# Local attention: the weighted product in front of masks and scores, masks as quarter products

## The reference

```python
q = l2norm(q) * qs;  k = l2norm(k) * ksc
q, k = rotary_xpos(q, k)
# windows of 64 queries; keys of the own window and of the one before
sim = einsum('bhwid,bhwjd->bhwij', bq, bk)
mask = (i < j) | (i > j + WINDOW) | (j == -1)
sim = where(mask, -finfo.max, sim)
attn = softmax(sim, axis=-1)
out = einsum('bhwij,bhwjd->bhwid', attn, bv)
x = x + out.reshape(b, n, INNER) @ wo
```

## Time and the profile before

| | before |
|---|---|
| median of three runs | 1756.01 us (1754.92 to 1756.5) |
| profiled execution, own time | 1755.7 us |
| its span, first to last instruction | 1753.9 us |
| mean granted TensorE clock | 0.991 |
| PE busy | 1674.9 us (95%) |
| PE weight loads (PEld) | 1154.1 us (66%) |
| DVE busy | 1446.5 us (82%) |
| ACT busy | 1299.2 us (74%) |
| POOL busy | 1039.0 us (59%) |
| DMA, mean | 54 GB/s |

### The profile page before, as it was taken

One profiled execution on the slowest core, in us unless ns is written; L12 is line 12 of the kernel. 1 busy time (PEld: TensorE's weight loads), 2 busy tenths in 40 slices (PEclk: granted clock), 3 DMA queues, 4 the chain that ended last, 5 costly groups with the idle time before them and its releaser, 6 DMA issues. The chain is left out here.

```text
span 1753.9 us, 54573 instructions
## 1 busy us (share of the span) xinstructions
PE 1674.9 (95%) x18245; PEld 1154.1 (66%) x18373; DVE 1446.5 (82%) x3283; ACT 1299.2 (74%) x3588; POOL 1039.0 (59%) x1015
## 2 busy tenths in 40 slices
PE   6999999979999999999989997999999999998997
PEld 4666666646777777777765664777777777775664
DVE  3777777769999999999967776899999999986996
ACT  5888888848998998989982224998998998985221
POOL 1333333337777777777763324777777777775664
PEclk9999999989999999999999999999999999999999
DMA  3211111111111111111113321111111111113443
GB/s 118 69 48 48 48 48 48 43 43 35 44 39 39 42 40 37 42 42 36 42 50 94 92 76 37 38 43 45 33 42 45 33 42 45 33 40 88 110 122 86
DMA packets 201095, 94.02 MB, mean 54 GB/s; under 512 B 82578, under 2 KB 192060, under 8 KB 201020
## 3 DMA queue, kind: packets, MB, share of 16 engines
q1 hardware_dynamic: 201020, 93.06, 20.1%
HBM read 51.00 MB, written 25.23 MB: 43 GB/s over the span
## 5 line engine op out<-in xcount | busy, mean ns | idle before, releaser
L846 ACT ACTIVATE pr<-banks,nb,rr 128x128 f32<-128x128 f32 x1024 | 456.3, 465 | 5.0 <-DVE nb L915 5.0
L747 POOL TENSOR_TENSOR rr<-ss,half_neg 128x16 f32<-128x16 f32 x128 | 374.4, 2925 | 19.0 <-POOL ss L744 17.0
L764 POOL TENSOR_TENSOR pr<-pr,rl 128x512 f32<-128x512 f32 x256 | 266.5, 1041 | 103.3 <-DVE rl L877 103.3
L885 DVE TENSOR_REDUCE ss<-sq 128x16 f32<-128x1024 f32 x128 | 156.1, 1219 | 75.4 <-ACT sq L795 61.3
L846 ACT ACTIVATION_READ_ACCUMULATOR pr<-banks,nb,rr 128x1 f32 x1024 | 216.5, 211 | 0.0
L1216 ACT ACTIVATE f_g<-banks,b_s 128x512 f32<-128x512 f32 (+1 forms) x96 | 65.9, 686 | 202.0 <-PE banks L1300 192.2
L893 DVE TENSOR_REDUCE mx<-banks 128x8 f32<-128x1024 f32 x128 | 156.0, 1219 | 9.0 <-PE banks L1022 8.3
L383 POOL TENSOR_SCALAR a_ve<-a_mv 128x2 f32<-128x2 f32 x96 | 21.4, 223 | 226.5 <-DVE a_mv L394 223.4
L755 POOL TENSOR_TENSOR krot<-ka,rr 128x512 f32<-128x512 f32 x128 | 134.4, 1050 | 22.3 <-POOL rr L747 11.7
L974 PE MATMUL banks<-ident,pr 128*128 128x128 f32 x1024 | 141.2, 281 | 5.9 <-POOL pr L764 5.9
L837 ACT COPY pT<-banks 128x512 f32<-128x512 f32 x128 | 75.1, 587 | 95.9 <-PE banks L974 95.9
(11 more groups left out here) (126 smaller groups left out, 4210.4 us busy)
## 6 DMA issues: line engine op xcount, KB each, us to landing
ve<-vt SPq DMA_DIRECT2D x128, 128.0 KB, 2.2
hs<-y_d SPq DMA_DIRECT2D x128, 64.0 KB, 2.0
yt<-y_d SPq DMA_DIRECT2D x64, 128.0 KB, 2.1
y_d<-yn SPq DMA_DIRECT2D x64, 128.0 KB, 2.0
f_h<-y_d SPq DMA_DIRECT2D x128, 64.0 KB, 2.0
f_y<-y_d SPq DMA_DIRECT2D x64, 128.0 KB, 2.2
xa<-in_L_attn_x SPq DMA_DIRECT2D x32, 128.0 KB, 2.2
xr<-in_L_attn_x SPq DMA_DIRECT2D x32, 128.0 KB, 2.3
```

Of the source, the lines that this page charges most:

```text
L747: nc.gpsimd.tensor_tensor(rr[:, r, :], ss[:, r, :], half_neg[:], ALU.pow).then_inc(T["rr"], 1)
L764: nc.gpsimd.tensor_tensor(pr[:, e], pr[:, e], rl[:, e].unsqueeze(2).broadcast_to([P, UH, P]), ALU.mult).then_inc(T[("ne", "no")[e]], 1)
L846: a = nc.scalar.activation(pr[:, e, j, :], bank[e][:, j * P:(j + 1) * P], ACT.Exp, bias=nb[:, X.t, UH * e + j:UH * e + j + 1], scale=rr[:, ...
L885: nc.vector.tensor_reduce(ss[:, 2 * X.p + X.t, :], sq[:].rearrange("p (h d) -> p h d", d=DH), AX.X, ALU.add).then_inc(T["ss"], 1)
```

## The change

`weigh` goes from lag 3, near the end of the slot, to lag 4, between `turn_h` and `scores`. In even tiles, where both windows' queries take the same values, one product of 128 columns takes the place of two of 64. The two mask products on the full array become four on quarters of it (64 rows, 64 columns, 512 columns of mask; the mask of one head is read four times by a broadcast), with the table laid out anew. `project_v` goes in front of `turn_k`.

```diff
--- before.py
+++ after.py
@@ window_masks
-    return np.ascontiguousarray(np.stack([np.tile(m, (1, UH)) for m in both], 1).astype(np.float32).reshape(P, -1))
+    per_half = np.stack([m.reshape(2, WIN, 2 * WIN) for m in both], 2).transpose(1, 0, 2, 3)
+    return np.ascontiguousarray(np.tile(per_half, (2, 1, 1, 1)).astype(np.float32).reshape(P, -1))
@@ build
-        masks_f = sb("masks_f", [P, TPB, UH * P])
-        masks = sb("masks", [P, TPB, UH * P], BF16)
+        masks_f = sb("masks_f", [P, 2, TPB, P])
+        masks = sb("masks", [P, 2, TPB, P], BF16)
@@ scores
                 until(pe, T["po"], X.x)
-                for e in range(2):
-                    nc.tensor.matmul(bank[e][:], ident_b[:], masks[:, X.t, :], start=True, stop=False,
-                                     skip_group_check=True)
+                apart(pe)
+                for w in range(2):
+                    for e in range(2):
+                        r = slice(64 * e, 64 * e + 64)
+                        nc.tensor.matmul(bank[e][64 * w:64 * w + 64, :].rearrange("p (j k) -> p j k", k=P),
+                                         ident_b[r, r], masks[r, w, X.t, :].unsqueeze(1).broadcast_to([WIN, UH, P]),
+                                         start=True, stop=False, skip_group_check=True)
@@ weigh
                 for j in range(UH):
-                    for w in range(2):
+                    for q in ((slice(0, P),) if X.t == 0 else (slice(0, WIN), slice(WIN, P))):
                         for e in range(2):
                             h = 2 * j + e
-                            early = vt[:, X.p, 0, h, :] if X.t == 0 else ve[:, X.p, h, :]
-                            m = nc.tensor.matmul(bank[4][64 * e:64 * e + 64, j * P + 64 * w:j * P + 64 * w + 64],
-                                                 vt[:, X.p, X.t, h, :] if w else early,
-                                                 pT[:, e, j, 64 * w:64 * w + 64], start=True, stop=True)
+                            keyed = ve[:, X.p, h, :] if q == slice(0, WIN) else vt[:, X.p, X.t, h, :]
+                            m = nc.tensor.matmul(bank[4][64 * e:64 * e + 64, j * P + q.start:j * P + q.stop],
+                                                 keyed, pT[:, e, j, q], start=True, stop=True)
@@ t_pe, the order
             turn_h(Tile(l, i, p, s, 0))
+            weigh(Tile(l, i, p, s, 4))
             scores(Tile(l, i, p, s, 2))
             turn_even(Tile(l, i, p, s, 3))
             turn_odd(Tile(l, i, p, s, 3))
...
             turn_q(Tile(l, i, p, s, 1))
             out_project(Tile(l, i, p, s, 4))
-            weigh(Tile(l, i, p, s, 3))
+            project_v(Tile(l, i, p, s, 1))
             turn_k(Tile(l, i, p, s, 1))
-            project_v(Tile(l, i, p, s, 1))
```

More of the change, by code:

```diff
@@ L183, in late_loads @@
                 load_late(sp, tabs[:].rearrange("p a t d -> p (a t d)"), tabs_c.ap() if hasattr(tabs_c, "ap") else tabs_c)
-                load_late(sp, masks_f[:].rearrange("p t d -> p (t d)"), mask_c.ap() if hasattr(mask_c, "ap") else mask_c)
+                load_late(sp, masks_f[:].rearrange("p w t d -> p (w t d)"), mask_c.ap() if hasattr(mask_c, "ap") else mask_c)
                 load_late(sp, wqkv_s[:], wqkv.rearrange("l p n -> p l n"))
```

## The result

The changed kernel takes 1758.23 us (median of 12, 1753.95 to 1759.94); the kernel before took 1755.18 us beside it. The ratio is 1.0016, 95% interval 1.0008 to 1.0023: slower, but by less than the 0.2% that I had named as the limit of telling. The forecast was 1757.7. It had started from 1756.0, so that the forecast change was +1.7 us; measured side by side it is +3.1. Medians are over all executions, of which one of four of e7_power_split took 4154 us (its median without that one is 1741.1) and one of the thirteen of the kernel before beside it 4512 us; the ratios leave these two out.

A forecast was written before the change was run, and what follows sets the result against it. TensorE sets the pace at 8.184 us a slot, with a VectorE-ScalarE ring of 8.16 limiting any gain. From 1756.0, +0.7 us for the loop and +1 for the layers' ends gave 1757.7 us, range 1747 to 1771.

The forecast's parts named there:

- The step that carried it: Attention loop: TensorE's own work falls from 8.18 to 7.79 us a slot, but project_v's wait for squares_q keeps the slot 8.19.
- both ways from there to the next peak: Loop rings from squares_q through project_v, one via turn_k and kT, one via weigh, masks and scores: 8.19 us each.
- turn_k to kT: Loop, TensorE to ScalarE: 0.71 us, four turns 0.60 and hop 0.11; a hop 0.06 shorter would make that ring 8.15.
- hole in TensorE: Before project_v in each loop slot: TensorE idles 0.3 us, waiting for squares_q to release the shared bank.
- One sign: Profile after the change: TensorE busy about 7.5 of 8.2 us a slot.
- The step from half the array to quarters: TensorE between weigh and masks: taken as 0.10 us, bounds 0 and 0.10, no row showing it.
- The loop term: Full attention slots: 8.19 against 8.184 us, +0.006 x 120 slots = +0.7 us.
- The end of the layers: Last weigh behind the first feed-forward transposes: +0.5 us at each of two layers, +1 us, bounds 0 and 2.
- The layers' starts: First slots of each layer: the prediction gave them no term of their own.
- A: Rival: the tie to squares_q does not bind; loop slot at the ring without TensorE, 8.10 to 8.12 us; 1748; chance 0.20.
- B: Rival: weigh to first score over 0.37 us, masks in pairs or dearer step; pairs +22, about 1778; chance 0.22.
- C: Rival: TensorE alone sets the loop's pace, 7.79 us a slot, 47 us saved, 1709; chance 0.04.

The follow-up runs named there:

- e7_power_split: Changed kernel with VectorE's add_q before sums and GpSimd's power split into a keys' and a queries' half; 1742.0 us, ratio 0.9918.
- e3: Changed kernel with VectorE's add_q moved in front of sums; 1745.0 us, ratio 0.9944.
- e5: Kernel before the change with only VectorE's add_q moved in front of sums; 1753.2 us, ratio 0.9986.
- e1: Changed kernel with project_v put back behind turn_k; 1796.6 us, ratio 1.0234.
- e2: Kernel before the change with only quarter masks and merged even-tile products, weigh and project_v left in place; 1747.0 us, ratio 0.9946.
- e6: Kernel before the change with quarter masks, merged even-tile products and add_q before sums; 1739.9 us, ratio 0.9912.
- e8: Kernel before the change with quarter masks, merged even tiles, add_q before sums and GpSimd's power in two halves; 1730.1 us, ratio 0.9846.
- e4: Changed kernel with the two old full-array mask products between weigh and scores; 1794.7 us, ratio 1.0224.
- e10: Changed kernel with weigh's 16 products of 64 columns in even tiles too; 1758.8 us, ratio 1.0023.
- e9: Changed kernel with the last weigh of each layer before the first feed-forward transposes; 1752.4 us, ratio 0.9987.

## Why the prediction was right, and where its terms were off

The step that carried it held: TensorE's own slot falls to about 7.8 us (8.18 from 710.24 to 718.42, less the hole of 0.31 and 0.10 for project_v's bare weight load), and nothing of that reaches the clock on the wall, since project_v waits for squares_q and both ways from there to the next peak cost a slot of 8.2. The waits in the profile and e3 beside e5 show it, and e1 shows what the wait buys. The single sizes, forecast and measured: hop from squares_q to project_v 0.05 and 0.05; project_v 0.97 and 0.96; turn_k to kT 0.71 and 0.71; quarter masks 0.27 and 0.24; mx to squares_q 3.45 and 3.45; hole in TensorE 0.3 and 0.31. One sign did not come: I had named a busy time of TensorE of about 7.5 us a slot, and it is 320.69/40 = 8.02. The modelled end of out_project (716.88) covers half of the hole, so busy time is no measure of it; the starts are.

The step from half the array to quarters costs what the other changes cost: in the slot above, weigh's last group starts at 711.31 and the first mask comes at 711.52, 0.21 later. In the kernel before, in a slot of the same parity, weigh's last group and turn_k on the full array stood as far apart:

```profile
711.75 0.29 PE L1090 MATMUL banks<-pT,vt 128*64 128x64 f32 x4
...
711.96 0.66 PE L974 MATMUL banks<-ident,krot 128*128 128x128 f32 x4
```

Groups of weigh follow each other by 0.12, so each of the two steps costs 0.09. The Trainium skill (TensorEngine Tiling (Array Packing), Key Properties) says that a change of the tiling mode drains TensorE; the trace agrees, in that the step between two parts of the array costs what the step to the full array does.

The loop term was mis-sized a little: +0.7 us was forecast for 120 slots, and it is (8.203 - 8.184) x 104 = +2.0. I had taken 8.19 by letting the shorter hop to kT count in part; it is 0.71 in three slots of four and 0.64 in the fourth. The slots take 8.18, 8.14, 8.19 and 8.30 in turn; the long one is that of the late nb, with 3.56 from mx to squares_q.

The end of the layers was mis-sized by more. I gave it +1 us, with 2 as the upper bound. From the last scores to the first feed-forward product the kernel before takes 13.5 and 13.3 us, the changed one 15.1 and 16.4, together +4.7. The order that I named, weigh behind the first feed-forward transposes, is part of it, but I counted only those transposes' 0.5 us, and neither that they can wait themselves nor the clock. End of layer 1 in the changed kernel (L1292 is the transposes):

```profile
1602.86 1.11 PE L1292 MATMUL banks<-ident,f_xn 128*128 128x128 f32 x4 [0.97 <-DVE f_xn L399]
...
1604.18 0.43 PE L1095 MATMUL banks<-pT,vt 128*64 128x64 f32 x4
1604.39 0.43 PE L1095 MATMUL banks<-pT,ve 128*64 128x64 f32 x4
```

TensorE stands 0.97 us for VectorE's f_xn with the last weigh queued behind. And it runs there at half clock, longer than before. The granted clock is the third figure from the end in these windows, from the last scores to the first feed-forward product; the changed kernel:

```profile
908.00:923.09 15.09, 11.46 (x128) 9.80 (x121) 7.62 (x29) 8.29 (x24) 5.90 (x8) 0.77 0.22 54
1592.02:1608.44 16.42, 11.75 (x129) 10.17 (x121) 8.33 (x31) 8.48 (x24) 5.89 (x8) 0.75 0.27 71
```

and the kernel before, at the end of layer 0:

```profile
910.10:923.57 13.47, 10.41 (x142) 9.21 (x141) 6.43 (x27) 8.50 (x25) 4.31 (x7) 0.87 0.17 40
```

It is 0.77 and 0.75 against 0.87 at both ends of the kernel before; at 1.2 GHz weigh's records come 0.21 apart in groups of four, against 0.12. The ends of the other runs part the two. At a granted clock of 0.87 or 0.88 an end takes 13.3 to 13.6 us with weigh first (the kernel before, e2, e5, e6, e8) and 14.1 to 14.3 with weigh behind the transposes (e1, e3, e4, e7, e10); at 0.75 to 0.78 it takes 14.1 to 14.3 with weigh first (e2, e8, e9) and 15.1 to 16.4 with weigh behind (the changed kernel, e1, e3, e10). So the order costs about 0.8 us an end at the same clock, 1.6 in all and within my bounds. Most of the other 3 us goes with the lower clock, which I had not counted at all. Both orders have ends at either clock, so the order does not settle it. It may still tilt it: over all executions the mean granted clock is 0.987 to 0.991 in the changed kernel and 0.991 to 0.993 in e9, which differs in this order alone. How the order does that stays open.

The layers' starts I had put at nothing, without a reason. There the changed kernel wins. Its first scores come 1.8 us earlier in layer 0, and in layer 1 they follow the first feed-forward product of layer 0 by 1.9 us less. In the first slot of a layer TensorE stands for krot, until 4.7 us after turn_q's start in either kernel. In the kernel before, project_v comes behind that wait, at half clock; start of layer 1:

```profile
1074.71 1.11 PE L974 MATMUL banks<-ident,krot 128*128 128x128 f32 x4 [4.03 <-POOL krot L755]
1075.61 1.92 PE L986 MATMUL banks<-wqkv_s,hT 128*128 128x512 f32 x2
...
1078.29 0.27 PE L1026 MATMUL banks<-kT,qT 64*64 64x64 f32 x2
```

In the changed kernel it is done inside the wait:

```profile
1071.51 1.12 PE L987 MATMUL banks<-wqkv_s,hT 128*128 128x512 f32 x2 [1.37 <-ACT sq L831]
1074.17 0.66 PE L975 MATMUL banks<-ident,krot 128*128 128x128 f32 x4 [1.54 <-POOL krot L756]
...
1075.95 0.34 PE L1031 MATMUL banks<-kT,qT 64*64 64x64 f32 x2
```

From turn_k to the first score it is 3.58 us before and 1.78 after (3.82 and 2.23 in layer 0). With the old masks (e4) it is 2.30, and with project_v behind turn_k (e1) 2.80, so both parts of the change have a share.

The two spans differ by 2.6 us: -3.7 at the starts, +1.0 from the first to the last scores of the layers (the loops' +2.0 are in it), +4.7 at the ends and +0.6 behind the last. So the nearness of 1757.7 to 1758.2 owes something to two misses of opposite sign, the layers' ends and their starts. The mechanism in the loop does not.

Of the rivals, A (the floor at 8.12) did not come; e2 shows that the floor is in fact 8.15, a few hundredths above my sum of the same ring. Just under it, at 8.09, lies the ring through krot, which no step of mine had summed up. B did not come, and e4 shows its price is real. C fell.

## What to carry to other kernels

When an engine is full in the profile, look how long the longest ring through the other engines is before saving work on it: the saving is worth only the difference. A move that fills one hole ties the moved step to what its operands and its bank wait for; count what is queued behind it, in the last slots too, where each wait is bare. Of a change with several parts try each alone: here the quarter masks by themselves give 0.5%, and moving weigh and project_v gives that back.

## What I had not expected of the hardware

Two elementwise operations on two operands in SBUF slow each other down when GpSimd and VectorE run them together, and it is the one that starts later that pays. In e7 share starts first, and add_q takes 1.25 us (mean 1.234 over 40). In e3 add_q starts first (706.87) and takes 0.65, and share, 0.15 behind it, takes 1.40 where it takes 1.04 in the changed kernel:

```profile
707.02 1.40 POOL L765 TENSOR_TENSOR pr<-pr,rl 128x512 f32<-128x512 f32 x1 [0.71 <-DVE rl L878]
```

The two products of share in e7 take 2.76 us together, and 2.76 - 2 x 1.04 = 0.68 is about one add_q, as if they took turns. The Trainium skill (SBUF — State Buffer, SBUF: two separate sides) has it that VectorE, when it reads two inputs from SBUF, and GpSimd share one pair of ports, which the one that starts first holds for its whole instruction. The trace agrees with it for share and add_q. It does not for power, which reads SBUF on GpSimd too: in the changed kernel add_q starts 0.6 to 0.8 us into power's 2.92 and takes 0.69. No run measured any of these by itself.

pow on GpSimd takes longer with more columns: 2.92 us for 16, 1.64 for 8. Four products on quarters of the array, each of 512 columns, are done in 0.24 us, up to the first score; two such on the full array take 0.54 with the step to quarters.
